# Accumulating graph tables by node: ScalarE copies groups out of PSUM, VectorE adds one column and does most products, three PSUM buffers

## The reference

```python
edge_index = jnp.stack([src, dst])
x = _layernorm(x + _L0_gnn_ref(x, L0_gnn_weight, L0_gnn_bias, src, dst), axis=-1)
x = _layernorm(x + _L1_gnn_ref(x, edge_index, edge_weight, L1_gnn_W1, ...), axis=-1)
x = _layernorm(x + _L2_gnn_ref(x, edge_index, L2_gnn_W1, ...), axis=-1)
x = _layernorm(x + _L3_gnn_ref(x, edge_index, edge_attr_96, L3_gnn_Wq, ...), axis=-1)
return x
```

## Time and profile before

| | |
|---|---|
| Times of three runs | 2393.83, 2395.80, 2396.03 us; median 2395.8 |
| The profiled execution's own time | its span, 2394.0 us from the first instruction to the last |
| Busy, of the span | TensorE 82%, VectorE 57%, ScalarE 42%, GpSimd 40% |
| Accumulation, 43.5 to 568 us | VectorE busy 513.2 of 524.5 us, TensorE 458.7, ScalarE 430.8 |
| Weighted passes, 670 to 1090 us | TensorE busy 420.0 of 420.0 us |
| Attention, 1310 to 2394 us | GpSimd busy 791.1 of 1084 us |

### The profile page before, as it was taken

The page is one execution under the profiler, slowest core; times in us unless marked ns, Lnnn a source line. Parts: engine busy times, 40 slices in busy tenths (PEclk is TensorE's granted clock), DMA queues, the critical chain, the costliest instruction groups (busy, mean ns, idle before and its releaser), DMA issues. The chain is left out here.

```text
span 2394.0 us, 46888 instructions
## 1 busy us (share of the span) xinstructions
PE 1970.0 (82%) x14784; PEld 1716.6 (72%) x14785; DVE 1371.8 (57%) x3363; ACT 999.8 (42%) x2697; POOL 954.4 (40%) x947
## 2 busy tenths in 40 slices
PE   7888888887999999999898477777777777777775
PEld 3666666665799999998786367676767676776765
DVE  6999999997720111442324455555555555555554
ACT  5788888885320000111213334343434343434432
POOL 3122222222000000000001477777777777777775
PEclk9999999998999999999998555555555555555555
DMA  1477766768888887785562575565555555555552
GB/s 55 82 110 129 114 115 110 127 117 197 265 312 288 293 290 285 284 297 192 179 226 87 153 183 162 159 166 155 162 162 161 161 159 163 160 162 156 160 158 64
DMA packets 225379, 416.45 MB, mean 174 GB/s; under 512 B 130818, under 2 KB 150296, under 8 KB 215448
## 3 DMA queue, kind: packets, MB, share of 16 engines
q1 hardware_dynamic: 186414, 334.76, 50.1%
q0 software_dynamic: 38784, 79.48, 12.7%
HBM read 347.71 MB, written 66.43 MB: 173 GB/s over the span
## 5 line engine op out<-in xcount | busy, mean ns | idle before, releaser
L2354 POOL DMA_INDIRECT attention_windowed_vkv<-kv_dram,ttention_windowed_vsrc x808 | 781.1, 967 | 247.0 <-issue 222.5
L2445 PE MATMUL attention_windowed_vps_e<-attention_windowed_vwe,attention_windowed_vattr 97*128 97x96 f32 x1616 | 403.7, 431 | 119.9 <-DVE ttention_windowed_vscore L2520 90.7
L2459 PE MATMUL attention_windowed_vps_s<-attention_windowed_hot,attention_windowed_vmsg 128*104 128x32 f32 x1616 | 319.8, 362 | 177.4 <-DVE attention_windowed_vmsg L2524 153.4
L2445 PEld LDWEIGHTS attention_windowed_vps_e<-attention_windowed_vwe,attention_windowed_vattr 97*128 97x128 f32 x1616 | 366.5, 332 | 125.6 <-issue 125.6
L2459 PEld LDWEIGHTS attention_windowed_vps_s<-attention_windowed_hot,attention_windowed_vmsg 128*104 128x104 f32 x1616 | 297.4, 289 | 208.9 <-DVE attention_windowed_vmsg L2524 180.1
L1273 PE MATMUL graph_layers_acc<-graph_layers_w_tab,graph_layers_g 125*96 125x125 f32 x3750 | 417.8, 269 | 0.0
L678 ACT ACTIVATE add_edges_hot_lo<-add_edges_hot_lo,parts 128x128 bf16<-128x128 bf16 x1212 | 371.4, 387 | 90.1 <-DVE add_edges_hot_lo L761 90.1
L1273 PEld LDWEIGHTS graph_layers_acc<-graph_layers_w_tab,graph_layers_g 125*96 125x96 f32 x3750 | 406.6, 163 | 0.1
L729 PE MATMUL add_edges_ps_four<-add_edges_hot,add_edges_hot_lo 128*128 128x200 bf16 x2424 | 332.0, 258 | 0.0
L1103 POOL CAST graph_layers_g<-graph_layers_w_tab 125x480 bf16<-125x480 f32 x4 | 2.3, 585 | 736.0 <-ACT graph_layers_w_tab L1150 730.0
L2387 ACT ACTIVATE attention_windowed_vmsg<-ttention_windowed_vscore 128x32 f32<-128x32 f32 x202 | 46.3, 229 | 595.1 <-DVE ttention_windowed_vscore L2520 595.1
(11 more groups left out here) (244 smaller groups left out, 2458.0 us busy)
## 6 DMA issues: line engine op xcount, KB each, us to landing
graph_layers_w_tab<-w_blocks SPq DMA_DIRECT2D x75, 1562.5 KB
graph_layers_c_tab<-c_blocks SPq DMA_DIRECT2D x56, 800.0 KB
attention_windowed_vattr<-in_attr_T SPq DMA_DIRECT2D x202, 192.0 KB, 2.7
attention_windowed_vdrow<-dstf_dram SPq DMA_DIRECT2D x202, 192.0 KB, 3.2
w_blocks<-strip SPq DMA_DIRECT2D x24, 1562.5 KB, 13.9
c_blocks<-add_edges_counts SPq DMA_DIRECT2D x24, 800.0 KB, 4.8
first_table<-c_blocks SPq DMA_DIRECT2D x19, 800.0 KB, 4.3
attention_windowed_vkv<-kv_dram,ttention_windowed_vsrc POOLq DMA_INDIRECT x808
```

What stands on the lines that cost most here:

```text
L2354: nc.gpsimd.indirect_dma_start(out=kv[s][:, k, :], out_offset=None, in_=kv_dram, in_offset=bass.IndirectOffsetOnAxis(ap=src4[s][:, k:k + 1 ...
L2445: nc.tensor.matmul(ps_e[s % BANKS][:, k, :], attr[:, s, k * P:(k + 1) * P], wes[:], start=True, stop=True)
L2459: last = nc.tensor.matmul(ps_s[s % 2], msg[s][:, k, :], hot[s][:, k, :], start=k == 0, stop=k == Q4 - 1)
```

## The change

`strip` is laid out by node: a column is now `[c, t]`, the 25 tiles of one node are contiguous, and so are the 20 nodes of a four (500 columns). With that:

- TensorE writes 200 contiguous columns a product. The first column of a four always starts at offset 0, so noughts are written only to columns 200 to 499 (L744). There are three PSUM buffers. The rounds of TensorE and ScalarE are written out.
- ScalarE copies nodes 1 to 19 of a four (475 columns of each table, 950 elements) over what is in the ring (`copy`, L666), and VectorE adds the first node alone (`add_column`, L830, 50 elements), since only that node can already hold a sum. GpSimd's clearing of blocks is gone but for the head and the end of the ring.
- ScalarE's products go from 12 to 4 a batch. VectorE does the third and the middle part whole (L804, L808) and half of the high part (`high`, L813), and `tiles` is written with the pair layout (L799).
- `convert` reads one tile's nodes 25 elements (100 bytes) apart and writes them contiguously.
- `w_blocks` and `w_tab` keep the order by node. L1273 therefore reads its 125 moving columns 100 bytes apart.
- `examine_edges` computes offsets times 25, also looks at the largest jump between fours, and does not clear the ring on ScalarE.

```diff
-        ps_four = [mem.ps(f"ps_four{s}", [P, 2, BANK]) for s in range(2)]
+        BANKS = 3
+        ps_four = [mem.ps(f"ps_four{s}", [P, 2, BANK]) for s in range(BANKS)]
         ps_odeg = mem.ps("ps_odeg", [P, NT + 1])
...
+        def by_tile(b, n):
+
+            first = (b % SLOTS_B * LANES + n * PIECE) * NT
+            return strip[:, 0, first:first + PIECE * NT].rearrange("p (c t) -> p t c", t=NT)
...
+            nc.gpsimd.memset(strip[:, :, OVERLAP], 0.0).then_inc(ends_clear, 1)
+            for b in range(0, NT - 2, SLOTS_B):
+                pool.wait_ge(folded, b // SLOTS_B + 1)
+                nc.gpsimd.memset(strip[:, :, OVERLAP], 0.0).then_inc(overlap_clear, 1)
+                pool.wait_ge(head_converted, b + 1)
+                pool.wait_ge(weights_stored[0], 16 * (b // SLOTS_B + 1))
+                nc.gpsimd.memset(strip[:, :, HEAD], 0.0).then_inc(ends_clear, 1)
...
+            def copy(q):
+
+                act.wait_ge(multiplied, q + 1)
+                if q > 0:
+                    act.wait_ge(copied, q)
+                nc.scalar.activation(strip[:, :, bass.ds(ats.pop(q) + NT, (REACH - 1) * NT)], ps_four[q % BANKS][:, :, NT:REACH * NT],
+                                     ACT.Copy).then_inc(copied, 1)
+
+            def scaled(g):
+
+                act.wait_ge(lo_ready, g + 1)
+                for j in range(BY_ACT, G):
+                    done = nc.scalar.activation(hot_lo[g % 2][:, 1, j, :], hot_lo[g % 2][:, 0, j, :], ACT.Copy, scale=parts[:, 0, g * G + j:g * G + j + 1])
+                done.then_inc(parts_ready, 1)
+
+            def convert(b, n):
 
                 if n == 0:
-                    act.wait_ge(block_done, r - 1)
-                    if reaches(r, 3):
-                        act.wait_ge(counts_stored, 16 * (r - 2))
-                some = slice(n * NT // 5, (n + 1) * NT // 5)
-                done = nc.scalar.activation(counts[:, some, 0:LANES], strip[:, 0, some, bass.ds((r + 2) % SLOTS_B * LANES, LANES)], ACT.Copy)
+                    act.wait_ge(block_done, b + 1)
+                    if b > 0:
+                        act.wait_ge(counts_stored, 16 * b)
+                done = nc.scalar.activation(counts[:, :, n * PIECE:(n + 1) * PIECE], by_tile(b, n), ACT.Copy)
+                if n == 0:
+                    done.then_inc(head_converted, 1)
                 if n == 4:
                     done.then_inc(converted, 1)
...
+                    if g >= 2:
+                        copy(2 * g - 3)
+                    scaled(g)
+                    if g >= 1:
+                        copy(2 * g - 2)
+                    if r >= 2:
+                        for n in CONVERT_AT[k]:
+                            convert(r - 2, n)
...
+            def batch(g):
+
+                s, at = g % 2, spots(g)
+                for u in range(2):
+                    q = 2 * g + u
+                    pe.wait_ge(hot_ready, q + 1)
+                    if u == 1:
+                        pe.wait_ge(parts_ready, g + 1)
+                    if q >= BANKS:
+                        pe.wait_ge(column_added, q - BANKS + 1)
+                    both = ps_four[q % BANKS]
+                    for table in range(2):
+                        nc.tensor.matmul(both[:, table, PLACES:NT * REACH], nought[:], noughts[:, PLACES:], start=True, stop=False)
+                    for m in range(Q4):
+                        e = Q4 * u + m
+                        cells = both[:, :, 0:PLACES] if m == 0 else both[:, :, bass.ds(at[e], PLACES)]
+                        nc.tensor.matmul(cells[:, 0], hot_lo[s][:, 0, e, :], hot[s][:, e, :], start=False, stop=m == Q4 - 1)
+                        last = nc.tensor.matmul(ps_odeg[:], hot_lo[s][:, 0, e, :], hot_hi[s][:, e, :],
+                                                start=g == 0 and e == 0, stop=g == NG - 1 and e == G - 1)
+                        if g == NG - 1 and e == G - 1:
+                            last.then_inc(odeg_ps, 1)
+                        for part in range(3):
+                            last = nc.tensor.matmul(cells[:, 1], hot_lo[s][:, 1 + part, e, :], hot[s][:, e, :],
+                                                    start=False, stop=m == Q4 - 1 and part == 2)
+                    last.then_inc(multiplied, 1)
...
+            def add_column(q):
+
+                dve.wait_ge(copied, q + 1)
+                if q > 0:
+                    dve.wait_ge(column_added, q)
+                cells = strip[:, :, bass.ds(ats.pop(q), NT)]
+                nc.vector.tensor_tensor(cells, cells, ps_four[q % BANKS][:, :, 0:NT], ALU.add).then_inc(column_added, 1)
...
+                        if g > 0:
+                            dve.wait_ge(multiplied, 2 * g)
                         lanes(g + 1, s)
...
+                    if g > 0:
+                        add_column(2 * g - 2)
                     if more:
                         tiles(g + 1, s)
                         third(g + 1, s)
+                        middle(g + 1, s)
+                    if g > 0:
+                        add_column(2 * g - 1)
+                    if k == 0 and r >= 2:
+                        b = r - 2
+                        dve.wait_ge(column_added, 2 * g)
+                        if b % SLOTS_B == 0:
+                            fold()
+                            dve.wait_ge(folded, b // SLOTS_B + 1)
+                        finish(b)
+                    if more:
+                        high(g + 1, s)
                         places(g + 1, s, 0)
...
-        w_tab = [mem.sb(f"w_tab{s}", [P, NT, LANES]) for s in range(W_SLOTS)]
+        w_tab = [mem.sb(f"w_tab{s}", [P, LANES, NT]) for s in range(W_SLOTS)]
...
-                    return nc.tensor.matmul(acc[j % 2][0:D, 0:L], g[(k - 1) % 2][0:L, t, :], w_tab[s][0:L, t, :], start=t == 0, stop=t == NT - 1)
+                    return nc.tensor.matmul(acc[j % 2][0:D, 0:L], g[(k - 1) % 2][0:L, t, :], w_tab[s][0:L, :, t], start=t == 0, stop=t == NT - 1)
```

More of the change, by code:

```diff
@@ new lines, in _, with columns @@
+            act.wait_ge(ends_clear, 1)
+            ats = {}
+            def columns(first, end):
+                why = "a node number less RING times the multiples of RING up to it, times the number of tiles"
+                _, at = nc.values_load_multi_w_load_instructions(ring_col[0:1, first:end], engines=(mybir.EngineType.Activation,),
+                                                                 min_val=0, max_val=(RING - 1) * NT, skip_runtime_bounds_check_because=why)
+                ats.update(zip(range(first, end), at))
@@ L735, in _ @@
+            for g in range(NG):
+                batch(g)
         @block.vector
@@ L792, in add @@
[L792 to L802 removed]
+                n = P // 2
@@ L810, in body @@
             def body(r, batches):
[L811 to L818 removed]
+                g0 = 4 * r - 2 + batches[0]
+                columns(max(0, 2 * g0 - 2), 2 * (g0 + len(batches)) - 2)
```

278 lines of the change are left out of this document (100 added, 178 removed).

## The result

The changed kernel takes 2813.8 us (median of four runs, 2810.2 to 2817.1), beside 2394.8 us for the kernel before (2389.4 to 2396.0). The ratio is 1.176, 95% interval 1.174 to 1.178: it is 17.6% slower. The prediction was 2347 us with a range of 2270 to 2745. It had the wrong sign, and the time lies above the range.

What follows compares the result with a forecast made beforehand. It took VectorE to bound the accumulation before, ScalarE after, and TensorE the weighted passes. -58 (accumulation) + 1 + 3.5 (ends) + 5 (far reads) = -48.5 on 2394.0 gave 2345.5, plus 1.8 to the median: 2347 us, range 2270 to 2745.

Steps and rivals of the forecast that it cites:

- The moving operand of L1273: Weighted passes, TensorE: reading the 125 moving columns 100 bytes apart was forecast to add 5 us, bounds 0 and 84.
- (a): Weighted passes: a far element takes about two port slots, so at most 6 ns more a record; +5 us taken.
- (b): Weighted passes: the fp32 column itself doubles, or a far element costs 1.9 ns on any engine; +321 to +490 us.
- Rival 1: Weighted passes: TensorE's far columns cost double, 107 ns more a record, +400 us, total 2742 us; chance 0.28.
- ScalarE's conversion: Accumulation: a piece of 625 elements read 100 bytes apart takes 1.36 us instead of 0.71.
- Rival 2: Accumulation: ScalarE's conversion costs no more than before, TensorE binds, gain 129 us instead of 58, total 2276 us; chance 0.12.
- ScalarE's sum of a round: Accumulation: products 4.7, copies 7.0, conversion pieces 6.3 and short waits make 18.2 us instead of 20.5; gain 58 us.
- I give this nothing: Accumulation: waits between engines, with copies up to a batch late, add nothing beyond ScalarE's own sum; 0 us.
- rival 3: Accumulation: the chain of waits binds, late ScalarE copies delay VectorE and TensorE; 2448 us at 1 us a batch; chance 0.10.
- VectorE and TensorE: Accumulation: their rounds take 14.8 and 15.3 us, below ScalarE's 18.2, so neither binds.
- the contiguous output: Accumulation, TensorE: writing products contiguously was given no gain; the rows left at most 8% for it.
- The ends: Before and after the accumulation: +1 us for more operations in `examine_edges`, +3.5 us for the final copy, conversion and casts.

## Why the prediction was wrong, step by step

**The moving operand of L1273** is the step that failed. I listed two readings and chose (a), "because the fp32 stream leaves every second slot of the port free": at most 84 us, 5 taken. Measured: 450 us, 231 instead of 111 ns a record. What holds is the last clause of (b), "a far element costs 1.9 ns on any engine": 231 / 125 = 1.85 ns, beside 1.88 and 1.87 ns in the rows of ScalarE and VectorE that I had used for the conversion. It is no rule for every operation, though: VectorE's casts of far fp32 to bf16 took 1.1 to 1.3 ns an element. I took two rows as an absolute time for one term and as a ratio of slots for the next, and nothing in the trace favoured the ratio; no run shows the free slots that (a) leaned on. The size taken for (a) was not its own either: 0.045 ns x 125 x 3750 is 21 us, and I took 5. Rival 1 had 0.28. The measured 450 us lies between its middle price of 400 and its upper one of 490, and the range ended at the middle one.

**ScalarE's conversion**: right. 1.41 us a piece against 1.36, with runs 0.73. Rival 2 falls.

**ScalarE's sum of a round**, 18.2 us: right as a sum; the round is 18.2 with aligned loads, and it fell by 2.8 us when the pieces became short. But it was 19.2, and the part where I wrote "I give this nothing" is where it went. 24 rounds x 1.0 us make 24 us, close to the 21 by which the gain ahead of the weighted passes fell short (33 instead of 53.5). The mechanism is rival 3's (a late start on one engine holds the products queued behind it), its cause was none that I named: a register load that the change moved from a multiple of 16 bytes to 4 and 8 bytes off. The order of the instructions showed the load at the head of a round, and I counted it at nothing because it was hidden before.

**VectorE and TensorE**: a column of 50 elements 0.20 us (forecast 0.21), a four 1.94 us from noughts to noughts (forecast 1.91). One column of a four takes 0.37 us, as in the earlier trace rows, so the contiguous output gave TensorE nothing. The rule of the Trainium skill on PSUM patterns that the prediction quoted (Advanced Engine Details and Errata, PSUM Cachelines) does not show in these products.

**The ends**: the last column was added at 532.3 us and the casts ended at 538.8, 6.5 us (forecast 7.7, before 4.2). The first `lanes` came 1.4 us later (forecast 1).

## What to carry to other kernels

A layout is paid for by every later reader. Ask first which engine reads the tensor most often and without a pause, and price its reads: here the accumulation saved 33 us once, and 3750 products of a stage that is all TensorE paid 120 ns each. When rows of two engines give the same absolute time for an access pattern, take that time for the third engine too before making up a ratio. Look at what the sequencers do between instructions (register loads, their addresses), since it shows as "issue" or is put down to another engine. And an idle GpSimd is no free hand beside a busy VectorE.

## What was not expected of the hardware

- VectorE's cast of far fp32 to bf16 costs little more than one of runs, if anything: 699 and 781 ns for 625 elements 100 bytes apart in the kernel after and 801 in the mean of 48 casts with two pieces on VectorE, beside 749 and 789 for runs. Its copy of far fp32 to fp32 takes 3764 ns for 1875, 1.9 to 2.0 ns an element, as on ScalarE (2613 ns for 1250: 2.0 to 2.1) and GpSimd (17.48 us for 9375: 1.86).
- A VectorE operation of 0.33 us stood still for 17.6 us while GpSimd made three copies back to back (17.5 us).
- A load of eight registers takes 0.54 to 0.61 us from a multiple of 16 bytes and 1.74 to 1.85 otherwise. Close behind the issue of the counts' store it took 1.0 us more on VectorE and 1.25 more on ScalarE (3.0 us); that the store is the reason was not tested.
- TensorE's far columns have a second rise from 18 to 24 elements (241 to 321 ns a record), and none at 25 (232). The fall of the granted clock to 0.50 within step 24 changed nothing in it.
